# Filler products in gaps of TensorE, another order in the feed-forward slots, and a cast moved to GpSimd

## Chip, cores and metric

One core of a Trainium2 chip. The metric is the device time of one execution in microseconds, by the median of several executions. The profile comes from one further execution.

## The reference

The input is 32 images of 56 x 56 pixels with 24 channels, in float32. What is computed on it, one step after another:

- a Swin block: layer normalization, attention in shifted windows of 7 x 7 with 3 heads of 8, residual; then layer normalization, an MLP 24 to 96 to 24 with gelu, residual;
- a gated convolution block: `x + silu(conv3x3(h @ w_in) + conv_b)`, where `h` is the normalized input;
- twice (layers 0 and 1): `t + mixer(ln(t))`, where the mixer is a product 24 to 48 with batch norm and relu, an FFT over the 3136 tokens, a diagonal complex product with relu, the inverse FFT and a product 48 to 24; then `t + ffn(ln(t))`, where the ffn is 24 to 96 to 24 with relu on numbers rounded to an 8-bit float (5 exponent bits, 2 mantissa bits), accumulated to a 16-bit one:

```python
h = jax.nn.relu(_qlinear(x, W1, b1))
y = _qlinear(h, W2, b2)
```

## The kernel before

The 32 images are eight "quads" of 4 images; the 4 images of a quad lie side by side on the 128 partitions (32 each, 24 of them channels), the tokens in the free dimension. The loop over the quads is written out for each engine (`for q in range(nq)`), and the order in every engine's queue is written by hand; engines meet through semaphores that count up. A quad goes through window attention, MLP, convolution, and for each of two layers `mixer` and `ffn`.

Almost every matmul is recorded at one line, L1124 (`mm`), so its groups are told apart by tiles. `blocks` makes a product with a block-diagonal matrix as two products of 64 x 64. A float32 product shows as two records, so that `x4` is one call of `blocks` or two filler products. The eight PSUM banks are `ps[:, 0..7]`.

**Layer normalization** is a pipeline over four engines: TensorE subtracts the mean with a matrix (`center`), ScalarE squares (L695, for pairs L693), TensorE sums the squares (`variance`), ScalarE takes logarithm (L707, for pairs L705) and exponential with -0.5 (L712), VectorE multiplies (L932, for pairs L940, `normed`). TensorE's waits for these are the gaps that the change is about.

**Fillers.** `keep_busy(bank, n)` issues n full products of 128 x 128 by 128 x 448 into a bank that nobody reads. Before, it is called in four places: once in `mixer` ahead of the wait for the last normalized tile, with 2 products in each layer, once in `ffn` before the first up product (2), and for each late slot of layer 0 (1).

**The head of window attention.** TensorE waits for the first windows' scores' inputs: keys masked by head on VectorE (L982). Later each row of windows needs the row maxima: turned by TensorE, copied by ScalarE (L763), and written by 4 DMAs of the SP queue (L510).

**MLP.** For each of 8 rows of windows, two up products (96 rows out), gelu on ScalarE (L778), a down product. The last row's normalization is made at `i == 1`, between the first row's up products and the others.

**Convolution.** Normalization over four pairs, 2 x 9 taps of 16 products in two groups of rows, silu as exponential, logarithm and exponential on ScalarE (L793, L799, L803), `move` that turns the images back, residual on VectorE, then the centering of the mixer's normalization, pair by pair (`center_mix`), and their variances.

**Feed-forward slots.** `ffn` runs in 10 slots for 7 tiles of 448 tokens. In slot s TensorE issues, in this order: the mixer's last product for tile s (bank 7, `ps<-area_hz,mix`; VectorE adds it to `xs`, L1073), the variance for tile s-1, the variance of a second normalization that runs along (in layer 0 that of the next mixer, three tiles behind, in layer 1 that of the next quad's windows, one behind), the down product for tile s-2 (waits for `f_hid` and for VectorE's add), the up products for tile s-1 (three, wait for `normed`), the centering for tile s, and the centering of the second normalization. ScalarE copies the three up products to float16 (L841), the down product too (L833); VectorE adds bias and rectifies (L1097), casts all three parts, 1344 elements a partition, to the 8-bit float (L1103, `f_hid`), adds the down bias (L1086) and the residual (L1090). `r16` has one buffer: the next tile's rectification waits for `f_hid`; `hq8` has two.

**GpSimd** zeroes areas and the convolution's border, copies the pixels from window order to image order during the MLP (L632), and in quad 0 makes the tables of the transform (L593, L597), which it stores by DMA. SP loads them back (L500). Its queue per quad: border, eight copies, `input_pads` twice, `zero_ring` when the layer 1 inverse stage begins, `ones_in_ring`, `zero_key_pads` at the end.

Of the kernel before, what the change touches and what calls it, by code (L numbers as in the profile page):

```python
# [85 lines left out]
def LN_FFN(l):  # L86
    return 4 + 2 * l
# [177 lines left out]
def build_kernel(nc, x, keep, raw, g2, g4, out, nq=NQ):  # L265
    ctx = ExitStack()
    with ctx:
# [271 lines left out]
        def _(gp):  # L539
# [68 lines left out]

            for q in range(nq):
# [29 lines left out]
                input_pads()  # L639
                gp.wait_ge(filled, q * FILLS + step_of(1, ST_I2))  # L640
# [4 lines left out]
                gp.wait_ge(ring_ready, 2 * q + 3)  # L645
                gp.wait_ge(filled, q * FILLS + FILLS)
# [215 lines left out]
        def _(ve):  # L862
# [202 lines left out]
            def ffn(q, l):  # L1065
                o = l * (HC + 1)
                for s in range(FFN_SLOTS):
# [23 lines left out]
                    if 0 <= s - 1 < NT:  # L1091
                        b, k = (s - 1) % 2, l * NT + s - 1
                        for m in range(HC):
                            ve.wait_ge(f_half, (q * 2 * NT + k) * HC + m + 1)
                            if m == 0 and k >= 1:
                                ve.wait_ge(f_hid, q * 2 * NT + k)
                            ve.tensor_scalar(r16[:, m, :], a16[:, b, m, :], fb[:, o + m:o + m + 1],  # L1097
                                             0.0, ALU.add, ALU.max).then_inc(f_relu, 1)
                        ve.wait_ge(f_relu, (q * 2 * NT + k + 1) * HC)
                        if k >= 2:  # L1100
                            ve.wait_ge(f_down, q * 2 * NT + k - 1)
                        ve.sem_inc(passed_ve, 1)
                        ve.tensor_copy(hq8[:, b, :, :], r16, saturate=False).then_inc(f_hid, 1)  # L1103
# [18 lines left out]
        def _(pe):  # L1122
# [67 lines left out]
            def window_attention(q):  # L1190
# [8 lines left out]

                pe.wait_ge(normed, q * LN_N + NW)  # L1200
# [101 lines left out]
            def mlp(q):  # L1302
                pe.wait_ge(w2_loaded, 16 * HC)
                for i in range(NW + 1):
                    if i < NW:
                        row = MLP_ORDER[i]
                        if i == 1:
                            pe.wait_ge(attended, q * NW + NW)
                            center(q, LN_WIN2, NW - 1, xw)
                            variance(q, LN_WIN2, NW - 1)  # L1310
                        pe.wait_ge(normed, ln_count(q, LN_AT[LN_WIN2, row]))
# [21 lines left out]
            def conv(q):  # L1333
# [59 lines left out]
                center_conv(3)  # L1393
                pe.wait_ge(border, q + 1)
# [18 lines left out]
                center_mix(0)  # L1413
                center_mix(1)
# [8 lines left out]
            def mixer(q, l):  # L1423
# [18 lines left out]
                keep_busy(5 if l else 1, 2)  # L1442
# [85 lines left out]
            def ffn(q, l):  # L1528
                for s in range(FFN_SLOTS):
                    if s < NT:  # L1530
# [15 lines left out]
                    if 0 <= s - 1 < NT:  # L1546
                        variance(q, LN_FFN(l), s - 1)
# [222 lines left out]
```

## Time and profile before

| what | value |
|---|---|
| time, median of 3 runs | 3570.37 us (3561.97 to 3577.15) |
| profiled execution, its time | 3580.5 us |
| its span | 3578.7 us |
| TensorE (PE) busy | 3075.6 us, 86% |
| VectorE (DVE) busy | 1806.6 us, 50% |
| ScalarE (ACT) busy | 1622.2 us, 45% |
| GpSimd (POOL) busy | 215.0 us, 6% |
| granted TensorE clock, mean | 0.962 of full speed |

The profile is one execution. Rows of stretches give the stretch, its length, each engine's busy time with its number of instructions, the mean granted clock (PEclk) as a share of 2.4 GHz, the share of the DMA engines and GB/s. A timeline gives start, length, engine, line, operation, out<-in, the number of merged instructions and, in brackets, the idle time before and what ended it. PE is TensorE. Quads begin their attention at 47, 511, 948, 1385, 1826, 2262, 2697 and 3136 us.

### The profile page before, as it was taken

The page shows a single profiled execution, that of the slowest core. Times are in us where ns is not written, and L with a number is a line of the kernel's source. Part 1 is how long each engine was busy: PE and PEld are TensorE (multiplying, and loading weights), DVE is VectorE, ACT ScalarE, POOL GpSimd, SP SyncE. Part 2 cuts the span into 40 slices and gives each one's busy share as a digit, 9 for nine tenths or more (in the row PEclk, how much of TensorE's full clock was granted, in tenths as well). Part 3 has the DMA queues.
Part 4 walks back from the last instruction along what each step waited for, and adds up shares of the span by engine and source line. Part 5 has one row for each costly group of instructions (what it writes and reads, how often), then busy time and mean ns, then how long its engine had stood idle before and what let it go on. Part 6 is the DMA issues. An engine that isn't in the chain of part 4 may idle for free.

```text
span 3578.7 us, 110016 instructions
## 1 busy us (share of the span) xinstructions
PE 3075.6 (86%) x48976; PEld 1956.8 (55%) x48976; DVE 1806.6 (50%) x2852; ACT 1622.2 (45%) x2883; POOL 215.0 (6%) x462
## 2 busy tenths in 40 slices
PE   6968889788898888988989889888889888888888
PEld 3536646467354574554745647547465464554744
DVE  5524555355643546445464445634556355553555
ACT  2542354533555425544355443453544535435344
POOL 4510000000000000000000000000000000000000
PEclk8989999999999999999999999999999999999999
DMA  2321000110001100110001100011000110001100
GB/s 78 66 49 49 2 15 4 49 31 2 16 19 40 25 2 16 32 41 10 2 16 32 49 2 2 17 50 31 2 2 17 50 31 1 5 14 32 31 1 15
DMA packets 31251, 84.81 MB, mean 24 GB/s; under 512 B 24818, under 2 KB 25954, under 8 KB 26930
## 3 DMA queue, kind: packets, MB, share of 16 engines
q1 hardware_dynamic: 29506, 72.56, 8.5%
q8 instruction: 395, 6.47, 0.8%
q0 software_dynamic: 1280, 5.21, 0.5%
q14 instruction: 70, 0.57, 0.1%
HBM read 61.70 MB, written 14.84 MB: 21 GB/s over the span
## 4 chain that ended last, share of the span: by engine, by line
PE 72%; ACT 11%; DVE 6%; issue 5%; SPq 4%; DMA 3%; ACTq 0%; DVEq 0%
PE ps L1124 72%; ACT rs L712 3%; ACT lv L707 3%; SPq L495 2%; DMA area_ty<-area_hz 2%; SPq L510 1%; DVE area_ty L932 1%; DMA area_hz<-f_all 1%; DVE xs L1090 1%; ACT area_ty L793 1%; ACT area_ty L799 1%; ACT sq L693 1%; DVE area_ty L1086 1%; DVE area_ty L1062 0%; ACT lv L705 0%
## 5 line engine op out<-in xcount | busy, mean ns | idle before, releaser
L1124 PE MATMUL ps<-area_hz 32*64 32x147 f32 (+2 forms) x7180 | 365.2, 290 | 92.0 <-DVE area_hz L982 31.8
L1124 PE MATMUL ps<-area_ty,area_hz 113*64 113x49 f32 (+1 forms) x10240 | 393.8, 250 | 25.9 <-DMA area_ty<-area_hz 24.1
L1124 PEld LDWEIGHTS ps<-area_hz 32*64 32x64 f32 (+2 forms) x7180 | 293.2, 157 | 199.0 <-issue 175.5
L817 ACT ACTIVATE area_hz<-ps 121x384 f32<-121x384 f32 (+2 forms) x256 | 129.5, 519 | 590.6 <-PE ps L1124 590.6
L1124 PEld LDWEIGHTS ps<-area_ty,area_hz 113*64 113x64 f32 (+1 forms) x10240 | 332.4, 135 | 108.0 <-issue 107.4
L1124 PE MATMUL ps<-sq,keep_sb 64*64 64x392 f32 (+1 forms) x1728 | 328.5, 553 | 65.6 <-ACT sq L693 49.0
L932 DVE TENSOR_TENSOR area_ty<-ps,rs 128x392 f32<-128x392 f32 (+2 forms) x304 | 198.3, 653 | 327.0 <-ACT rs L712 326.9
L965 DVE TENSOR_REDUCE area_hz<-ps 113x12 f32<-113x588 f32 x256 | 196.7, 770 | 287.2 <-PE ps L1124 286.4
L1124 PE MATMUL ps<-area_ty,g_sb 56*112 56x192 f32 (+1 forms) x3712 | 311.5, 321 | 26.0 <-DVE area_ty L1062 19.7
L1124 PEld LDWEIGHTS ps<-area_ty,g_sb 56*112 56x112 f32 x3712 | 293.0, 173 | 44.7 <-issue 44.0
L1062 DVE COPY area_ty<-ps 120x896 f32<-120x896 f32 (+1 forms) x192 | 164.8, 858 | 255.8 <-PE ps L1124 255.8
L707 ACT ACTIVATE lv<-ps 128x448 f32<-128x448 f32 (+1 forms) x304 | 157.0, 517 | 275.4 <-PE ps L1124 275.4
L729 ACT ACTIVATE area_ty<-ps 113x588 f32<-113x588 f32 x256 | 168.8, 659 | 227.1 <-PE ps L1124 224.0
L817 ACT ACTIVATE area_ty<-ps 120x896 f32<-120x896 f32 (+1 forms) x192 | 140.2, 730 | 258.0 <-PE ps L1124 258.0
L1124 PE MATMUL ps<-xs,keep_sb 64*64 64x448 f32 (+1 forms) x1184 | 213.6, 538 | 47.1 <-DVE xs L1090 33.9
L1124 PEld LDWEIGHTS ps<-sq,keep_sb 64*64 64x64 f32 x1728 | 89.8, 138 | 288.4 <-ACT sq L695 122.4
L695 ACT ACTIVATE sq<-ps 128x448 f32<-128x448 f32 (+1 forms) x304 | 161.0, 529 | 177.0 <-PE ps L1124 172.2
L1124 PE MATMUL ps<-area_ty,ffn 128*128 128x448 fp8e5 x672 | 166.0, 355 | 86.2 <-DVE area_ty L932 81.9
L712 ACT ACTIVATE rs<-lv 128x448 f32<-128x448 f32 (+2 forms) x368 | 223.7, 608 | 32.7
L1124 PE MATMUL ps<-keep_sb,area_hz 112*58 112x56 f32 (+1 forms) x6144 | 196.2, 229 | 19.1 <-ACT area_hz L817 16.1
L1124 PEld LDWEIGHTS ps<-keep_sb,area_hz 112*58 112x58 f32 (+1 forms) x6144 | 193.6, 141 | 22.2 <-issue 22.1
L1124 PE MATMUL ps<-g_sb,area_ty 122*64 122x112 f32 (+1 forms) x3584 | 175.1, 259 | 12.5 <-issue 12.5
(123 smaller groups left out, 4078.9 us busy)
## 6 DMA issues: line engine op xcount, KB each, us to landing
area_hz<-f_all SPq DMA_DIRECT2D x16, 2541.0 KB
xw<-x_in SPq DMA_DIRECT2D x8, 1568.0 KB, 6.4
y_out<-xs SPq DMA_DIRECT2D x32, 252.0 KB
f_all<-piece POOLq DMA_DIRECT2D x16, 317.6 KB, 3.3
area_ty<-area_hz SPq DMA_DIRECT2D x256, 4.6 KB
area_hz<-raw_in SPq DMA_DIRECT2D x1, 2894.0 KB, 9.7
g_sb<-g_in SPq DMA_DIRECT2D x6, 355.2 KB
g_sb<-g_in SPq DMA_DIRECT2D x2, 710.5 KB
```

Source lines behind the costliest of these rows:

```text
L495: sp.dma_start(g4_sb[r + HALF * g:r + HALF * (g + 1), :, g, :], g4[r:r + HALF, :, :]).then_inc(tables_loaded, 16)
L510: sp.dma_start(qm[RW * j + 28:RW * j + 29, t % 3, :, :].rearrange("p w (h n) -> p (w h) n", n=L), mxt[NW * NH * g:NW * NH * g + NW * NH, t ...
L693: act.activation(halves(sq[:, k % 2, :]), pair_banks(i), ACT.Square).then_inc(squared, 1)
L695: act.activation(sq[:, k % 2, 0:w], ps[:, center_bank(k), 0:w], ACT.Square).then_inc(squared, 1)
L707: act.activation(lv[:, k % 2, 0:w], ps[:, variance_bank(k), 0:w], ACT.Ln).then_inc(logged, 1)
L712: act.activation(rs[:, k % 2, 0:w], lv[:, k % 2, 0:w], ACT.Exp, scale=-0.5).then_inc(root, 1)
L729: act.activation(pt[0:SIDE, n % 2, :, :], ps[0:SIDE, 2:4, 0:6 * L], ACT.Exp).then_inc(exped, 1)
L817: act.activation(dst, src, ACT.Relu if st in (ST_H, ST_F2) else ACT.Copy).then_inc(sc_kept, 1)
L932: ve.tensor_tensor(o, a, b, ALU.mult, **kw).then_inc(normed, 1)
L965: ve.tensor_reduce(mx[0:SIDE, u % 2, :].rearrange("p (g c r) -> p g c r", g=2, c=4)[:, :, k % 4], ps[0:SIDE, score_bank(k):score_bank(k) + ...
L1062: ins = ve.tensor_copy(dst, src)
L1124: return pe.matmul(o, a, b, start=start, stop=stop)
```

## The change

- `keep_busy` is called in five more places or with more products: 3 products at the head of window attention (quads 1 to 7), 1 and 2 in the MLP's step `i == 1`, 3 in the convolution after the last centering (behind a wait for the first pair's logarithm), 3 between the first two centerings of the mixer's normalization, and 4 for 2 in layer 0 of `mixer`. These are 14 products of a quad.
- In `ffn`, the variance for tile s-1 stands ahead of the mixer product for tile s.
- The cast of the rectified product moves from VectorE to GpSimd (`hidden_fp8`), with the same waits; layer 0's seven casts stand behind the second `input_pads`, layer 1's seven between the ring and the zeroing of the key columns.

```diff
--- before.py
+++ after.py
@@ -606,6 +606,16 @@
                 gp.memset(xhc[:, 0, HW + 1:64], 0.0)
                 gp.tensor_copy(xhc[:, 0, HW:HW + 1], spike[:, :]).then_inc(extra, 1)
 
+            def hidden_fp8(q, l):
+
+                for i in range(NT):
+                    k = l * NT + i
+                    gp.wait_ge(f_relu, (q * 2 * NT + k + 1) * HC)
+                    if k >= 2:
+                        gp.wait_ge(f_down, q * 2 * NT + k - 1)
+                    gp.sem_inc(passed_gp, 1)
+                    gp.tensor_copy(hq8[:, i % 2, :, :], r16, saturate=False).then_inc(f_hid, 1)
+
             for q in range(nq):
                 gp.wait_ge(attended, q * NW + NW)
                 gp.sem_inc(passed_gp, 1)
@@ -637,12 +647,14 @@
                 gp.wait_ge(filled, q * FILLS + step_of(0, ST_I1))
                 gp.sem_inc(passed_gp, 1)
                 input_pads()
+                hidden_fp8(q, 0)
                 gp.wait_ge(filled, q * FILLS + step_of(1, ST_I2))
                 gp.sem_inc(passed_gp, 1)
                 zero_ring()
                 gp.wait_ge(pads_ready, 3 + q + 1)
                 ones_in_ring()
                 gp.wait_ge(ring_ready, 2 * q + 3)
+                hidden_fp8(q, 1)
                 gp.wait_ge(filled, q * FILLS + FILLS)
                 gp.sem_inc(passed_gp, 1)
                 zero_key_pads()
@@ -1096,11 +1108,6 @@
                                 ve.wait_ge(f_hid, q * 2 * NT + k)
                             ve.tensor_scalar(r16[:, m, :], a16[:, b, m, :], fb[:, o + m:o + m + 1],
                                              0.0, ALU.add, ALU.max).then_inc(f_relu, 1)
-                        ve.wait_ge(f_relu, (q * 2 * NT + k + 1) * HC)
-                        if k >= 2:
-                            ve.wait_ge(f_down, q * 2 * NT + k - 1)
-                        ve.sem_inc(passed_ve, 1)
-                        ve.tensor_copy(hq8[:, b, :, :], r16, saturate=False).then_inc(f_hid, 1)
 
             for i in range(NW):
                 scale_windows(0, LN_FIRST, i)
@@ -1197,6 +1204,8 @@
                                  still[r, w, :], moving[r, w, :])
                     return ins
 
+                if q >= 1:
+                    keep_busy(2, 3)
                 pe.wait_ge(normed, q * LN_N + NW)
                 if q == 0:
                     pe.wait_ge(su_ve, N_SETUP_VE + 2)
@@ -1305,9 +1314,11 @@
                     if i < NW:
                         row = MLP_ORDER[i]
                         if i == 1:
+                            keep_busy(4, 1)
                             pe.wait_ge(attended, q * NW + NW)
                             center(q, LN_WIN2, NW - 1, xw)
                             variance(q, LN_WIN2, NW - 1)
+                            keep_busy(5, 2)
                         pe.wait_ge(normed, ln_count(q, LN_AT[LN_WIN2, row]))
                         for p in range(2):
                             u = 2 * i + p
@@ -1391,6 +1402,8 @@
                 variance_pair(LN_CONV, 1)
                 pe.wait_ge(mlp_added, q * NW + NW)
                 center_conv(3)
+                pe.wait_ge(logged, ln_count(q, LN_AT[LN_CONV, 0]))
+                keep_busy(0, 3)
                 pe.wait_ge(border, q + 1)
                 pe.wait_ge(normed, ln_count(q, LN_AT[LN_CONV, 1]))
                 tap(0, 0)
@@ -1411,6 +1424,7 @@
                     ins = tap(1, n)
                 ins.then_inc(conved, 1)
                 center_mix(0)
+                keep_busy(2, 3)
                 center_mix(1)
                 variance_pair(LN_MIX(0), 0)
                 move(1)
@@ -1439,7 +1453,7 @@
                 f3 = K("f3").rearrange("p (r n) -> p r n", r=2)
                 if l == 0:
                     pe.wait_ge(normed, ln_count(q, LN_AT[LN_MIX(0), 0]))
-                keep_busy(5 if l else 1, 2)
+                keep_busy(5 if l else 1, 2 if l else 4)
                 pe.wait_ge(normed, ln_count(q, LN_AT[LN_MIX(l), NT - 1 if l else NP - 1]))
                 pe.wait_ge(extra, q * 2 + l + 1)
                 for j in range(ST_STEPS[ST_H]):
@@ -1527,6 +1541,8 @@
 
             def ffn(q, l):
                 for s in range(FFN_SLOTS):
+                    if 0 <= s - 1 < NT:
+                        variance(q, LN_FFN(l), s - 1)
                     if s < NT:
 
                         if s >= 3:
@@ -1543,8 +1559,6 @@
                         pe.wait_ge(normed, ln_count(q, LN_AT[LN_WIN1, 0]))
                         pe.wait_ge(f_half, (q + 1) * 2 * NT * HC)
                         first_keys(q + 1)
-                    if 0 <= s - 1 < NT:
-                        variance(q, LN_FFN(l), s - 1)
                     if l == 0 and 0 <= s - 3 < NT:
                         variance(q, LN_MIX(1), s - 3)
                     if l == 1 and 0 <= s - 1 < NW:
```

## Rows read from the trace of the kernel before

**Rows 1.** Page, part 4; and the chain of waits, 196 to 290 us: start, us, what.

```profile
PE 72%; ACT 11%; DVE 6%; issue 5%; SPq 4%; DMA 3%; ACTq 0%; DVEq 0%
...
232.72 41.43 DMA area_hz<-f_all
```

**Rows 2.** Stretches of gelu, quads 1 and 7, and sum over quads 1 to 7.

```profile
633.56:651.78 18.22, 16.83 (x111) 3.83 (x108) 4.38 (x7) 12.15 (x16) 5.08 (x21) 0.72 0.42 92
...
3264.66:3280.04 15.38, 14.58 (x111) 3.78 (x108) 3.89 (x7) 12.15 (x16) 5.12 (x21) 0.89 0.51 109
sum 119.07, PE 110.41 PEld 27.51 DVE 29.80 ACT 85.45 POOL 35.72; mean PE 15.77 PEld 3.93 DVE 4.26 ACT 12.21 POOL 5.10
```

**Rows 3.** Stretches of the convolution, quad 7, and sum over quads 1 to 7.

```profile
3288.98:3308.85 19.87, 19.63 (x628) 11.08 (x631) 5.91 (x8) 8.24 (x10) 0.00 (x0) 1.00 0.02 4
sum 152.17, PE 145.45 PEld 80.60 DVE 41.39 ACT 57.70 POOL 0.00; mean PE 20.78 PEld 11.51 DVE 5.91 ACT 8.24 POOL 0.00
```

**Rows 4.** Stretches from the convolution to the mixer, sum over quads 1 to 7.

```profile
sum 132.79, PE 75.11 PEld 20.98 DVE 69.88 ACT 99.61 POOL 0.00; mean PE 10.73 PEld 3.00 DVE 9.98 ACT 14.23 POOL 0.00
```

**Rows 5.** Stretches of the mixer's first product, layer 0: quad 2, and sum.

```profile
1138.78:1148.93 10.15, 9.46 (x224) 9.29 (x225) 3.90 (x7) 3.43 (x7) 0.00 (x0) 1.00 0.02 4
...
sum 79.34, PE 74.46 PEld 73.34 DVE 27.32 ACT 24.02 POOL 0.00; mean PE 10.64 PEld 10.48 DVE 3.90 ACT 3.43 POOL 0.00
```

**Rows 6.** Stretch of window attention, quad 2.

```profile
947.95:1064.51 116.56, 110.40 (x2240) 73.81 (x2241) 63.93 (x85) 51.19 (x97) 0.00 (x0) 0.97 0.02 5
```

**Rows 7.** TensorE in order of time at the gaps: start, us, what [idle before].

```profile
1385.28 2.96 PE L1124 MATMUL ps<-area_hz 32*64 32x147 f32 x48 [3.53 <-DVE area_hz L982]
...
1503.19 0.88 PE L1124 MATMUL ps<-xw,keep_sb 64*64 64x392 f32 x4 [1.07 <-DVE area_ty L932]
...
1507.44 0.90 PE L1124 MATMUL ps<-area_ty,w 32*96 32x392 f32 x4 [1.91 <-DVE area_ty L932]
...
1533.84 0.97 PE L1124 MATMUL ps<-area_ty,wconv 32*32 32x392 f32 x16 [3.35 <-issue]
...
1563.04 1.22 PE L1124 MATMUL ps<-sq,keep_sb 64*64 64x392 f32 x8 [4.20 <-ACT sq L693]
...
1571.97 1.77 PE L1124 MATMUL ps<-keep_sb 128*128 128x448 f32 x4
1576.09 2.21 PE L1124 MATMUL ps<-mix,area_ty 64*64 64x96 f32 x36 [2.35 <-DVE area_ty L940]
```

**Rows 8.** Feed-forward slots: timelines of TensorE, ScalarE, VectorE, then the chain.

```profile
1354.61 0.96 PE L1124 MATMUL ps<-area_hz,mix 112*32 112x448 f32 x8
1355.50 1.63 PE L1124 MATMUL ps<-sq,keep_sb 64*64 64x448 f32 x8
...
1354.08 1.14 ACT L695 ACTIVATE sq<-ps 128x448 f32<-128x448 f32 x2
...
1355.67 0.68 DVE L1073 SCALAR_TENSOR_TENSOR xs<-ps,bn_bias,xs 128x448 f32<-128x448 f32 x1
...
1227.09 2.78 PE ps L1124 x16
...
1234.04 2.78 PE ps L1124 x16
...
1352.39 4.10 PE ps L1124 x23
...
1358.64 4.10 PE ps L1124 x23
```

**Rows 9.** Groups of GpSimd by shape: busy us, mean ns, idle before.

```profile
L593 POOL TENSOR_TENSOR piece<-terms,turns 121x672 f32<-121x672 f32 x32 | 45.9, 1455 | 49.0 <-DMA f_all<-piece 48.9
L597 POOL TENSOR_TENSOR piece<-piece 121x672 f32<-121x672 f32 x16 | 28.0, 1750 | 1.3
L632 POOL COPY xs<-xw 128x343 f32<-128x343 f32 x56 | 27.7, 495 | 123.7 <-issue 74.7 <-DVE xw L1022 49.0
L632 POOL COPY xs<-xw 128x28 f32<-128x28 f32 x56 | 11.6, 207 | 0.0
```

## Prediction

> **What bounds the kernel now.** I read the page first. The chain that ended last lies 72% on TensorE, with ScalarE and VectorE filling most of the rest: TensorE's stream, and the short waits inside it, set the time [rows 1]. That stream's speed depends on the granted clock, which is either 2.4 or 1.2 GHz. So the second view was stretches of one stage in quads 1 to 7, each with its mean granted clock as a share of 2.4 GHz. For a stretch of length T and mean clock c, the time at 1.2 GHz is 2(1-c)T. The gelu stretch of the MLP takes 18.22 us at 0.72 (10.2 us of it at 1.2 GHz) and 15.38 us at 0.89 (3.4 us) [rows 2]: 2.84 us for 6.8 us of low clock, or 0.42 us for each. The convolution takes 19.87 us with none [rows 3], and the first transform product of the mixer's layer 0 10.15 us with none [rows 5]. Third, TensorE's timeline, for what stands before such stretches: it idles 3.53 us before attention, 1.07 and 1.91 us in the MLP's head, 3.35 us before the taps, 4.20 us inside the second normalization and 2.35 us before the mixer [rows 7]. Fourth, one feed-forward slot. In layer 1 the mixer's last product (it fills bank 7) stands between the centerings and the variance at 1354.61, and the variance starts 0.89 us later at 1355.50, although the square it needs began at 1354.08 [rows 8].
>
> **Quad 0** gets nothing from the fillers: its mixer waits for the load of the table, 41 us that end at 274.15 [rows 1], so I count quads 1 to 7 for them and all eight for the slots.
>
> **Fillers, the cost.** One filler product is half of 1.77 us: two took that at 1571.97 [rows 7], so 0.88 us, 0.83 to the next start. Three before attention, 2.5 us, stand in 3.53 us of idleness that VectorE's masking ends; one (0.8) in 1.07, two (1.7) in 1.91; three (2.5) in 3.35, behind a wait for a logarithm that has ended when TensorE gets there; three (2.5) in 4.20; and two more (1.7) in 2.35 [rows 7]. All end before what ends the wait today, the closest with 0.2 us to spare. Cost: nothing. If a filler ran at 1.2 GHz it would take about 1.7 us instead of 0.8, and the three in the convolution would overrun by 1.7 us; fourteen in each of seven quads, all exposed, would be 7 x 14 x 0.83 = 81 us. I take 0 and keep a few us for the range.
>
> **Fillers, the gain,** if the clock stays at 2.4 GHz behind them. The full-clock length is subtracted from the sum over seven quads.
> - Gelu: 15.38 less 3.4 x 0.42 is 13.95; 119.07 - 7 x 13.95 = 21 us [rows 2]. ScalarE is busy 12.15 us of it, so a shorter floor than that isn't to be had.
> - Convolution: 152.17 - 7 x 19.87 = 13 us [rows 3]; 12 taken.
> - From there to the mixer: 132.79 us for seven, and 99.61 of it are ScalarE's [rows 4]. TensorE is not the bound, so I give half of the gelu rate, 0.2 us for each us, and 3.4 us of low clock a quad make 0.7 us: 4 us for seven, rounded down. Bounds 0 and 10.
> - First mixer product of layer 0: 79.34 - 7 x 10.15 = 8 us [rows 5].
> - Attention: one quad took 116.56 us at 0.97, 7.0 us of low clock, worth at most 2.9 us at the gelu rate [rows 6]. It has further waits, for the rows of maxima that come by DMA, that no filler is put into. I take 1 us a quad, 7 us; bounds 0 and 20.
> The sum is 52 us, with bounds 0 (no drop prevented) and 72. A change in the drops at other places, where the mixer's inverse stage starts, is not to be expected.
>
> **The slots.** Layer 1, one slot, with the order new. The square that begins at 1354.08 (two take 1.14 us) lets the variance start at 1354.71 instead of 1355.50. From the variance's start to the up products it is 3.14 us (1358.64 - 1355.50), which would give 1357.85. But the mixer product now follows the variance, 1355.51 to 1356.47, and VectorE adds it (0.68) until 1357.25, ahead of the normalization's scale in its order [rows 8]; that costs the scale 0.1, so 1357.94: 0.7 us less. Some is given back. The second variance is 0.9 us later against the first, so ScalarE reaches the second logarithm, the half-precision copies and the next square 0.23 us later, and the down product waits for the add. Followed round again the slot settles at 5.9 us instead of 6.25: four slots of 0.35, a first one of 0.6, a last one and the head that lose 0.3: **1.7 us a quad**. Layer 0: a slot is 6.95 us (1227.09 to 1234.04) and its loop goes through the second normalization: its variance now stands behind the mixer product, so its logarithm is 0.57 us later against the first variance, of the 0.89 us taken off: 0.32 gained, three times, 0.4 once before; the first, the last and the head lose 0.8 together, since there the square is not earlier or no mixer product was between: **0.5 us a quad**. Over eight quads 2.2 x 8 = 17 us. Bounds: 0 and 0.7 us for each of 96 slots, 67 us.
>
> **The cast.** It leaves VectorE, on whose queue nobody waits just behind it: in the new order the add that follows comes later still. Gain 0. On GpSimd the trace shows no cast. Its copies take 495 ns for 343 elements and 207 for 28: 0.91 ns an element and 0.18 us; 1344 elements would be 1.41 us. Its products of two tensors take 1455 and 1750 ns for 672: 2.9 and 3.5 us for 1344 [rows 9]. The bounds are a gain of 0 (a faster cast than 1.4 us has nobody waiting for it) and the cost at 3.5. I take 1.41, by the rows with one input and the same kind of operation. What waits for it is the down product of the next slot. In the layer 1 slot the rectifications end 2.6 us after the up products begin, the down product starts at 5.2: a cast of up to 2.1 us costs at most 5 us in all, at the tail; at 2.4 the slots still end 7 us under today's, at 2.9 they cost 30 us over today's, at 3.5 some 85 us. GpSimd's own queue: the zeroing of the key columns now stands behind the last cast, which ends 3 us before attention starts and takes 0.6; the zeroing of the ring (5.2 us) comes before the layer 1 slots. Both hidden.
> Weighed against a rule: the rows give GpSimd's copies 0.91 ns an element with one input [rows 9]. The Trainium skill, GPSIMD Engine Reference, section 3.1, gives 2.6 cycles an element at 1.2 GHz for elementwise work, which would be an estimated 2.9 us here; section 4.1 of the same page calls one-input work about line rate. By the first the slots would lose 30 us, by the second they gain 17; the first is rival 2.
> A second: in the rows the copies of GpSimd's setup vary, the in-place sum averages 1750 ns against 1455 for the product of the same size [rows 9], which a neighbour on VectorE may cause. The Trainium skill, SBUF - State Buffer, section Who interferes with whom, says that the two engines lock each other out of a shared port when VectorE reads two SBUF tensors. In my slot the cast (2.8 to 4.2 us after the up products) meets only VectorE's add from PSUM, so I charge nothing.
>
> **The sum.** 52 + 17 = 69 us off the profiled execution (3580.5 us, 3578.7 of them its span): 3511. The median of the runs, 3570.4, lies 10 us below that execution, so the forecast is 3502 us, 1.9% less.
>
> **Rivals.**
> 1. The fillers don't hold the clock, or it falls a few us later: only the slots' 17 us are left, 3553. For: the convolution's mean of 21.74 against 19.87 in quad 7 says that the same waits are not always followed by a drop, so more than their length counts [rows 3]. Against: what is left of each wait is 0.2 to 1.7 us. Chance 0.10.
> 2. The cast takes about 2.9 us, like the product of two tensors: the slots turn from -17 to +30, and the fillers' 52 stay: 3548. Chance 0.09.
> 3. Slower: the cast on the path of the next down product. From about 3.5 us (85 us on the slots, less 52) the kernel is slower, by 33 us: 3603; at 3.9 us it would be 3650. Place: TensorE waiting for GpSimd in front of each down product. For: the in-place sum's 2.6 ns an element would do it. Against: every one-input row. Chance 0.08.
> Forecast: 0.73.
>
> **The numbers.** A difference of 0.5% (18 us) is what a measurement of this kernel can tell from none. Faster by more: the forecast and most of rival 2, 0.73 + 0.09 = 0.82. Within: 0.10 (rival 1 lies on its edge). Slower: 0.08. The forecast's own range is 3478 (72 us from the fillers, 20 from the slots) to 3530; taken on to rivals 1 and 2 it is 3478 to 3554, which leaves rival 3 and the ends out.
>
> **What would show it.** Right: gelu stretches near 14 us with clock near 1.00, conv near 19.9, the mixer's first product at 10.15 in all quads, up products 5.9 us apart in layer 1 and 6.6 in layer 0, casts of 1.4 us on GpSimd, and no idle time on TensorE ended by GpSimd. Wrong: casts over 2.4 us; gaps after the fillers that end later than now; the clock still at 1.2 GHz in the gelu stretch.

## The result, and the profile after

The changed kernel takes 3513.0 us by the median of four runs, beside 3573.2 us for the kernel before (four runs as well, one more than the 3570.4 us of the forecast's table): a ratio of 0.984, with a 95% interval of 0.981 to 0.987. It is faster, by 1.6%; the forecast was 3502 us, 1.9% less, with a range of 3478 to 3554. The profiled execution's span fell from 3578.7 to 3515.2 us, 63.5 us.

First the page of the changed kernel, parts 1 and 4. `mm` is now line L1131.

```profile
PE 3115.1 (89%) x49194; PEld 1970.0 (56%) x49194; DVE 1704.2 (48%) x2740; ACT 1625.4 (46%) x2883; POOL 359.9 (10%) x574
...
PE 72%; ACT 12%; DVE 5%; issue 5%; SPq 4%; DMA 3%; ACTq 0%; DVEq 0%
```

The chain still lies 72% on TensorE, as in [rows 1]. TensorE is busy for 39.5 us more although the span is shorter. The 109 added filler products would be an estimated 90 us by 0.83 us each; the rest of its work takes some 50 us less, because less of it runs at 1.2 GHz. VectorE is busy for 102 us less and GpSimd for 145 us more, and VectorE's share of the chain went from 6 to 5%. The mean granted clock rose from 0.962 to 0.980.

Then the stages, as rows of stretches like those of [rows 2 to 6] (stretch, length, busy time and number of instructions of PE, PEld, DVE, ACT and POOL, granted clock, DMA share, GB/s). The gelu stretches of quads 1, 2 and 6, and the sum over quads 1 to 7:

```profile
631.08:646.45 15.37, 13.98 (x111) 3.64 (x108) 4.38 (x7) 12.14 (x16) 5.12 (x21) 0.89 0.50 109
1061.63:1075.44 13.81, 12.66 (x111) 3.82 (x108) 4.21 (x7) 12.14 (x16) 5.13 (x21) 1.00 0.56 121
...
2777.95:2794.61 16.66, 15.74 (x111) 4.11 (x108) 3.98 (x7) 12.14 (x16) 5.11 (x21) 0.80 0.47 100
...
sum 102.63, PE 94.35 PEld 26.33 DVE 29.56 ACT 84.99 POOL 35.81; mean PE 13.48 PEld 3.76 DVE 4.22 ACT 12.14 POOL 5.12
```

Four of seven quads run at 13.8 us and full clock. Quads 1, 4 and 6 still have 3.4, 3.4 and 6.8 us at 1.2 GHz (such a time is called a drop below). The convolution, quad 5 and the sum:

```profile
2368.38:2390.49 22.11, 20.73 (x628) 10.95 (x630) 5.91 (x8) 8.24 (x10) 0.00 (x0) 1.00 0.02 4
...
sum 143.71, PE 136.91 PEld 78.27 DVE 41.39 ACT 57.69 POOL 0.00; mean PE 19.56 PEld 11.18 DVE 5.91 ACT 8.24 POOL 0.00
```

The clock is 1.00 in all seven, yet quads 1, 3, 5 and 7 take 20.7 to 22.1 us, the others 19.8 or 19.9. From the convolution to the mixer, the sum; then the sum of the mixer's first product in layer 0:

```profile
sum 123.81, PE 94.21 PEld 30.65 DVE 70.04 ACT 99.63 POOL 0.00; mean PE 13.46 PEld 4.38 DVE 10.01 ACT 14.23 POOL 0.00
...
sum 71.06, PE 66.19 PEld 65.06 DVE 27.32 ACT 24.02 POOL 0.00; mean PE 9.46 PEld 9.29 DVE 3.90 ACT 3.43 POOL 0.00
```

Both stages are the same in every quad now (17.68 to 17.70, and 10.15 or 10.16). Attention, sum over quads 1 to 7, which was 819.45 us before (121.92 of them in quad 7, which takes 114.88 us now):

```profile
sum 812.00, PE 764.12 PEld 511.34 DVE 447.58 ACT 358.75 POOL 0.00; mean PE 109.16 PEld 73.05 DVE 63.94 ACT 51.25 POOL 0.00
```

TensorE in order of time, at the gaps of [rows 7] (what stands in brackets is the idle time that is left and what ended it):

```profile
1365.25 1.23 PE L1131 MATMUL ps<-area_hz 32*64 32x147 f32 x32 [1.27 <-DVE area_hz L994]
...
1084.38 0.95 PE L1131 MATMUL ps<-area_ty,wconv 32*32 32x392 f32 x32 [0.90 <-issue]
...
1109.92 0.89 PE L1131 MATMUL ps<-sq,keep_sb 64*64 64x392 f32 x8 [1.59 <-ACT sq L705]
...
1121.93 1.29 PE L1131 MATMUL ps<-mix,area_ty 64*64 64x96 f32 x26 [0.86 <-DVE area_ty L952]
```

Each of these gaps keeps idle time that the same instruction as before ends, and the MLP's head, from the end of attention to the gelu stretch, takes 6.80 us in both kernels: at full clock the fillers delay nothing. Last the slots. Stretches of layer 0's slots in quads 2 and 6, and one of layer 1's, of the kernel before (first fence) and of the changed one (second), each with the sum over eight quads:

```profile
1206.45:1264.47 58.02, 45.88 (x223) 12.67 (x223) 32.85 (x63) 34.53 (x70) 0.00 (x0) 1.00 0.00 1
...
sum 465.48, PE 370.46 PEld 102.11 DVE 262.84 ACT 276.54 POOL 0.00; mean PE 46.31 PEld 12.76 DVE 32.85 ACT 34.57 POOL 0.00
...
2209.26:2261.68 52.42, 42.73 (x230) 13.00 (x231) 32.18 (x65) 35.31 (x75) 0.60 (x1) 1.00 0.09 21
...
sum 423.25, PE 340.18 PEld 103.30 DVE 256.47 ACT 282.16 POOL 4.82; mean PE 42.52 PEld 12.91 DVE 32.06 ACT 35.27 POOL 0.60
```

```profile
1188.43:1245.57 57.14, 45.49 (x222) 12.56 (x222) 26.18 (x56) 34.88 (x70) 9.13 (x7) 1.00 0.00 1
...
2907.58:2966.12 58.54, 48.16 (x222) 13.12 (x223) 26.20 (x56) 34.99 (x70) 9.12 (x7) 0.94 0.00 1
sum 463.98, PE 376.52 PEld 103.10 DVE 209.61 ACT 279.57 POOL 72.99; mean PE 47.07 PEld 12.89 DVE 26.20 ACT 34.95 POOL 9.12
...
2173.17:2224.79 51.62, 45.72 (x237) 13.71 (x237) 25.95 (x58) 35.44 (x75) 9.69 (x8) 1.00 0.09 21
...
sum 415.57, PE 362.72 PEld 107.80 DVE 206.56 ACT 282.98 POOL 77.50; mean PE 45.34 PEld 13.48 DVE 25.82 ACT 35.37 POOL 9.69
```

At full clock layer 0 gains 0.9 us a quad and layer 1 0.8. But of layer 0's eight stretches five now have 3.4 or 6.8 us at 1.2 GHz; before, two had 3.4. GpSimd's casts, as the group of its line that answers to [rows 9]:

```profile
L617 POOL CAST area_ty<-area_ty 128x1344 fp8e5<-128x1344 f16 x112 | 146.1, 1305 | 870.2 <-DVE area_ty L1109 870.2
```

**Where the 63.5 us come from,** stage by stage: gelu 16.4, convolution 8.5, from there to the mixer 9.0, first product 8.3, attention 7.4, together 49.6; the slots 1.5 and 7.7 over eight quads; in quads 1 to 7 the rest of layer 0's mixer 4.1, where two fewer quads have a drop at the inverse stage (one for three), and layer 1's mixer -0.5 (five with a drop in both kernels). That is 62.4, and the rest is in quad 0.

### The profile page after: what moved, and what is told of

The parts are those of the page before. It is cut to its first block, busy times and chain, and to the rows that moved or that the text cites. A ratio compares the mean times of both kernels' runs of the same rounds, so it can differ in the third digit from the quotient of the medians.

```text
span 3515.2 us, 110460 instructions
## 1 busy us (share of the span) xinstructions
PE 3115.1 (89%) x49194; PEld 1970.0 (56%) x49194; DVE 1704.2 (48%) x2740; ACT 1625.4 (46%) x2883; POOL 359.9 (10%) x574
## 4 chain that ended last, share of the span: by engine, by line
PE 72%; ACT 12%; DVE 5%; issue 5%; SPq 4%; DMA 3%; ACTq 0%; DVEq 0%
PE ps L1131 72%; ACT lv L719 2%; SPq L495 2%; ACT rs L724 2%; ACT area_ty L853 2%; DMA area_ty<-area_hz 1%; ACT sq L707 1%; SPq L510 1%; DMA area_hz<-f_all 1%; DVE xs L1102 1%; ACT area_ty L845 1%; ACT sq L705 1%; DVE area_ty L1098 1%; ACT area_ty L805 1%; ACT area_ty L811 1%
## 5 line engine op out<-in xcount | busy, mean ns | idle before, releaser
L1131 PE MATMUL ps<-area_hz 32*64 32x147 f32 (+2 forms) x7180 | 357.7, 285 | 84.7 <-DMA area_hz<-f_all 28.8
L1131 PE MATMUL ps<-area_ty,area_hz 113*64 113x49 f32 (+1 forms) x10240 | 393.5, 250 | 22.1 <-DMA area_ty<-area_hz 20.1
L1131 PE MATMUL ps<-sq,keep_sb 64*64 64x392 f32 (+1 forms) x1728 | 335.1, 531 | 71.0 <-ACT sq L707 44.0
L1131 PEld LDWEIGHTS ps<-area_hz 32*64 32x64 f32 (+2 forms) x7180 | 287.8, 154 | 191.2 <-issue 168.7
L1131 PEld LDWEIGHTS ps<-area_ty,area_hz 113*64 113x64 f32 (+1 forms) x10240 | 332.0, 135 | 104.1 <-issue 103.5
L1131 PE MATMUL ps<-area_ty,g_sb 56*112 56x192 f32 (+1 forms) x3712 | 311.8, 321 | 26.0 <-DVE area_ty L1074 19.7
L1131 PEld LDWEIGHTS ps<-area_ty,g_sb 56*112 56x112 f32 x3712 | 293.3, 173 | 44.7 <-issue 44.0
L1131 PE MATMUL ps<-xs,keep_sb 64*64 64x448 f32 (+1 forms) x1184 | 219.8, 542 | 63.1 <-DVE xs L1102 48.0
L1131 PEld LDWEIGHTS ps<-sq,keep_sb 64*64 64x64 f32 x1728 | 84.1, 133 | 297.0 <-ACT sq L707 135.5
L617 POOL CAST area_ty<-area_ty 128x1344 fp8e5<-128x1344 f16 x112 | 146.1, 1305 | 870.2 <-DVE area_ty L1109 870.2
L1131 PE MATMUL ps<-keep_sb,area_hz 112*58 112x56 f32 (+1 forms) x6144 | 196.8, 229 | 17.7 <-ACT area_hz L829 16.0
L1131 PEld LDWEIGHTS ps<-keep_sb,area_hz 112*58 112x58 f32 (+1 forms) x6144 | 193.9, 141 | 21.1 <-issue 20.8
L1085 DVE SCALAR_TENSOR_TENSOR xs<-ps,bn_bias,xs 128x448 f32<-128x448 f32 x112 | 76.6, 684 | 233.7 <-PE ps L1131 233.7
```

What stands on the lines that cost most here:

```text
L617: gp.tensor_copy(hq8[:, i % 2, :, :], r16, saturate=False).then_inc(f_hid, 1)
L1085: ve.scalar_tensor_tensor(xs[:, sl], ps[:, 7, 0:TT], bn_bias[:, l:l + 1], xs[:, sl], ALU.add, ALU.add).then_inc(ve_kept, 1)
L1131: return pe.matmul(o, a, b, start=start, stop=stop)
```

## Experiments

**The theory** is the prediction's: the fillers hold the clock, the order in the slots gives a little, the cast gives nothing. **Rivals:** the order or the cast brings more than that; or drops are not prevented but only moved.

### The three parts, each alone or taken back

`e1_order` is the kernel before with only the variance put first:

```diff
                 for s in range(FFN_SLOTS):
+                    if 0 <= s - 1 < NT:
+                        variance(q, LN_FFN(l), s - 1)
...
-                    if 0 <= s - 1 < NT:
-                        variance(q, LN_FFN(l), s - 1)
```

> The kernel before with the variance ahead of the mixer product alone. My theory, corrected by the trace of after: the feed-forward stages of layer 0 shorten from 58.0 to about 57.2 us and those of layer 1 from 52.4 to about 51.7, 1.5 us a quad, 12 us in all (ratio 0.9967), and the granted clock stays where it was (0.96). Rival, that the order gives nothing by itself and the fillers made the whole gain: ratio 1.000. Rival, that the slots pay the whole 0.7 us they save at first order: 96 x 0.7 = 67 us, ratio 0.981.

Measured: 0.998 (0.997 to 0.999), 3563.5 us beside 3570.9. Two of its layer 0 slot stretches, quads 6 and 7, and the sum over eight:

```profile
2946.38:3005.09 58.71, 48.32 (x222) 13.13 (x223) 32.20 (x63) 35.03 (x70) 0.00 (x0) 0.94 0.00 1
3381.95:3439.10 57.15, 45.49 (x223) 12.59 (x223) 32.21 (x63) 34.91 (x70) 0.00 (x0) 1.00 0.00 1
sum 467.87, PE 382.37 PEld 104.57 DVE 257.76 ACT 280.00 POOL 0.00; mean PE 47.80 PEld 13.07 DVE 32.22 ACT 35.00 POOL 0.00
```

In quad 7, at full clock, the order takes 58.02 to 57.15, as in the changed kernel; layer 1 is 51.63 in six quads. So the order alone is worth 0.87 + 0.79 = 1.7 us a quad, 13 us. But seven of eight layer 0 stretches now have low clock in their last slots, and their sum is higher than before (467.87 us for 465.48). By the slots of this execution 4.9 us are left of the 13; by the medians the order is worth 7.3 us. So about half of its gain goes through the clock. That step was missing from the prediction.

`e2_cast` is the kernel before with only the cast moved (`hidden_fp8` on GpSimd, the five lines out of VectorE's):

> The kernel before with the cast on GpSimd alone. Theory: the cast was waited for by nobody and still is not, 0 us (ratio 1.000), casts of 1.3 us, feed-forward stages of 58.0 and 52.4 us unchanged except for up to 0.3 us at the tail of layer 1. Rival, that the move helps by freeing VectorE (98 us less busy): ratio below 0.998. Rival, that the later cast delays the down products: ratio above 1.002.

Measured: 1.000 (0.999 to 1.001). The slot stretches at full clock stay at 58.01 and 52.43 us. VectorE had nobody waiting behind the cast. `e4_cast_back` takes the cast back from the changed kernel:

> The kernel after with the cast back on VectorE. Theory: within 5 us of after (ratio to before about 0.984), since in the new order the add of the mixer product comes long after the cast in either place; if anything the tails are 0.1 us shorter. Rival, that the cast on VectorE holds up the add or the scale in the shorter slots: feed-forward stages longer by 0.3 us or more a slot-loop, ratio 0.99 or more.

Measured: 0.986 (0.984 to 0.988), 3517.8 us; its slots take 57.18 and 51.61 us at full clock, within 0.04 us of the changed kernel's. The cast's place is worth nothing in either kernel.

`e3_fill` is the kernel before with all fillers and nothing else:

```diff
+                if q >= 1:
+                    keep_busy(2, 3)
...
+                            keep_busy(4, 1)
...
+                            keep_busy(5, 2)
...
+                pe.wait_ge(logged, ln_count(q, LN_AT[LN_CONV, 0]))
+                keep_busy(0, 3)
...
+                keep_busy(2, 3)
...
-                keep_busy(5 if l else 1, 2)
+                keep_busy(5 if l else 1, 2 if l else 4)
```

> The kernel before with the five filler places alone. Theory: they carry some 45 us of the 60 (ratio about 0.987), the time at 1.2 GHz in gelu, convolution and up to the mixer's first product falls to some 10 us or less over the quads 1 to 7, and no gap ends later than before. Rival, that the fillers only pay with the shorter slots, or that the order pays most: ratio 0.995 or more.

Measured: 0.988 (0.986 to 0.990), 3524.3 us, 47 us less, with a clock of 0.983. Its sums: gelu 101.4, convolution 142.7, to the mixer 123.8, first product 71.1, attention 809.4, none above the changed kernel's by more than 0.1. This part carries four fifths of the change. The drops themselves can be counted: in each of the three traces without the new fillers (the kernel before, `e1_order`, `e2_cast`) all seven quads have one at the gelu stretch, and there are 15 to 17 from there to the end of the mixer's first product. With the fillers the gelu stretch has 3 (this run and the changed kernel), 0 (`e4_cast_back`) and 1 (`e5_cast_twice`, at its end), and from there on there are 0 or 1.

### How much filler it takes

`e11_one` is the changed kernel with one product in each place instead of three, two, three and three, and three instead of four in the mixer.

> The kernel after with 1 product instead of 3, 2, 3 and 3 in its filler places and 1 more instead of 2 in the mixer (the first MLP filler stays). Theory: what the clock answers to is how much of a wait is left idle, so with 2.5 us and more left in the waits before attention, in the convolution and in the second normalization the drops come back there, in about half of the quads, and the ratio to before lies between after's 0.984 and the order's 0.998, near 0.990. Rival, that any product in the gap is enough: 0.984.

Measured: 0.990 (0.988 to 0.992), clock 0.973. Its sums of gelu, of the convolution and from there to the mixer:

```profile
sum 108.60, PE 99.61 PEld 26.08 DVE 30.11 ACT 85.00 POOL 35.76; mean PE 14.23 PEld 3.73 DVE 4.30 ACT 12.14 POOL 5.11
...
sum 146.94, PE 140.01 PEld 80.39 DVE 41.37 ACT 57.71 POOL 0.00; mean PE 20.00 PEld 11.48 DVE 5.91 ACT 8.24 POOL 0.00
...
sum 131.95, PE 87.42 PEld 24.95 DVE 69.86 ACT 99.62 POOL 0.00; mean PE 12.49 PEld 3.56 DVE 9.98 ACT 14.23 POOL 0.00
```

From the convolution to the mixer nearly the whole gain is gone (131.9 against 123.8, and 132.8 in [rows 4]); gelu keeps 10 of 16 us, the convolution 5 of 8. So one product is not enough in any of the three, but how much it brings differs: much in gelu, where it takes the place of two, nearly nothing ahead of the mixer, where it takes the place of three.

### The cast doubled

`e5_cast_twice` is the changed kernel with one more copy of 1344 elements on GpSimd (121 partitions, into `twin`, a part of a tile that nobody needs then) ahead of each cast:

```diff
+                    gp.wait_ge(f_hid, max(1, q * 2 * NT + k)) if q or k else None
...
+                    gp.tensor_copy(twin, r16[0:121].rearrange("p m n -> p (m n)"))
                     gp.tensor_copy(hq8[:, i % 2, :, :], r16, saturate=False).then_inc(f_hid, 1)
```

> The kernel after with a copy of the same 1344 elements on GpSimd ahead of each cast (into an area nobody reads), so that the cast is ready 1.3 us later. Theory of rivals 2 and 3 of the prediction: the down product waits from about 2.1 us on; at 2.65 us the slots lose about 3 us a quad against after, 25 us in all (ratio to before about 0.991), and TensorE's idle time shows GpSimd as releaser. Rival, that there is more slack than I worked out: within 5 us of after (0.984). Rival, that every slot pays the copy in full: 96 x 1.3 = 125 us, ratio 1.02.

Measured: 0.984 (0.982 to 0.986), the changed kernel's own ratio. By the total the copies would cost nothing. The groups of GpSimd and one layer 1 slot stretch say otherwise:

```profile
L621 POOL CAST area_ty<-area_ty 128x1344 fp8e5<-128x1344 f16 x112 | 146.4, 1307 | 0.0
L620 POOL COPY piece<-area_ty 121x1344 f16<-121x1344 f16 x112 | 146.3, 1307 | 751.8 <-DVE area_ty L1113 751.8
```

```profile
2174.07:2226.87 52.80, 45.55 (x236) 13.74 (x237) 26.13 (x58) 35.68 (x75) 18.46 (x15) 1.00 0.09 22
```

Layer 1's slots take 52.80 against 51.62 us, alike in quads 1 to 6; layer 0's 57.44 against 57.14 in the one quad at full clock. That is 1.5 us a quad, some 12 us. The 12 us came back elsewhere: attention 807.6 (812.0), gelu 99.1 (102.6), layer 1's mixer, all quads, 537.1 (541.8), where two inverse stages have a drop and not six. Whether the copy has a part in that, or only chance, no run shows. An edit of 10 us can't be priced by the total while drops are about; stretches at full clock can. The prediction's curve gave 25 us for a cast of 2.6 us: too steep.

### The drops that are left

Two more edits go after them. `e6_tail` puts more fillers in the last slots of layer 0, and takes bank 0 for them instead of 4:

```diff
-                    if l == 0 and s > NT:
-                        keep_busy(4, 1)
+                    if l == 0 and s >= NT:
+                        keep_busy(0, 2 if s == NT + 1 else 1)
```

> The kernel after with filler products in the last slots of layer 0: 1 where there was none (slot 7) and 2 for 1 (slot 8). In after the clock falls there in 5 of 8 quads. Theory: those drops go, the layer 0 stage is 57.15 us in all quads instead of 58.0 on average, 5 to 8 us less than after (ratio to before about 0.982). Rival, that the fillers delay the centerings behind them: layer 0 stages above 57.2 at full clock.

`e7_more` adds to it one filler in the wait for the MLP's first gelu and one in two rows of attention:

```diff
+                            if u == 3:
+                                keep_busy(6, 1)
...
+                        if q >= 1 and n in (0, 4):
+                            keep_busy(5, 1)
```

> e6 and two more places: one filler between the two up products of the MLP's second row (a wait of 0.63 us for gelu, so it overruns by 0.2) and one ahead of the first two waits for rows of maxima in window attention. Theory: gelu stretches 14.0 us in all quads (three of after's were 15.4 to 16.7), attention 114 to 115 us instead of 116 on average: 10 to 15 us less than e6 (ratio to before about 0.978). Rival, that what makes the clock fall in gelu are the narrow products and not the waits: the drops stay, ratio as e6.

Measured: `e6_tail` 0.980 (0.979 to 0.982), `e7_more` 0.979 (0.977 to 0.981), clock 0.988. The layer 0 slots of `e6_tail`, sum over eight quads, then the gelu stretch of `e7_more`, quad 6 and sum:

```profile
sum 457.33, PE 375.95 PEld 106.59 DVE 209.56 ACT 279.03 POOL 73.00; mean PE 46.99 PEld 13.32 DVE 26.20 ACT 34.88 POOL 9.12
```

```profile
2760.22:2774.28 14.06, 13.54 (x113) 3.97 (x110) 4.21 (x7) 12.16 (x16) 5.12 (x21) 1.00 0.54 116
...
sum 98.46, PE 94.80 PEld 27.80 DVE 29.47 ACT 85.16 POOL 35.74; mean PE 13.54 PEld 3.97 DVE 4.21 ACT 12.16 POOL 5.11
```

All eight slot stretches are at 57.2 and full clock: fillers hold it there as well, and 6.7 us come back (463.98 to 457.33). More came than was looked for: layer 1's mixer, the next stage, takes 532.4 us for 541.8, since none of its eight inverse stages has a drop in this execution, where six had. `e7_more` has the same fillers there and two drops, so this second part isn't sure. In the gelu stretch the filler costs 0.25 us at full clock (14.06 for 13.81) and takes away what was left, 102.6 to 98.5. The two in attention did little: 806.8 us beside 808.3 in `e6_tail`, 115.3 a quad, where 114 to 115 were expected, and the intervals of the two versions overlap.

`e8_inverse` goes on from `e7_more`, with a filler ahead of the inverse stage:

```diff
+                pe.wait_ge(ve_kept, q * VE_FILLS + vector_fills(step_of(l, ST_F2, FOLDS)))
+                keep_busy(0, 1)
```

> e7 and one filler product between the last forward and the first inverse transform product of each mixer, in a wait of about 1 us that VectorE and ScalarE end. In after the clock falls there in 9 of 16 mixers, 1.55 us each. Theory: it falls no more, the stretches from the first transform product to the feed-forward slots take 56.35 us in both layers instead of 57.3 on average in e7, 10 us less in all (ratio to before about 0.976). Rival, that the narrow products of the inverse stage and not the wait bring the clock down there: unchanged, or slower by 16 x 0.1 us.

Measured: 0.981 (0.979 to 0.983), no better. TensorE in order of time at that place, first in `e7_more`, then in `e8_inverse`:

```profile
1156.07 1.03 PE L1131 MATMUL ps<-area_ty,g_sb 56*112 56x96 f32 x16 [0.39 <-issue]
1158.10 4.12 PE L1131 MATMUL ps<-keep_sb,area_hz 112*64 112x56 f32 x83 [1.01 <-ACT area_hz L829]
```

```profile
1157.36 1.03 PE L1131 MATMUL ps<-area_ty,g_sb 56*112 56x96 f32 x16 [0.39 <-issue]
1159.27 1.02 PE L1131 MATMUL ps<-keep_sb 128*128 128x448 f32 x2 [0.88 <-DVE area_hz L1067]
1160.22 2.99 PE L1131 MATMUL ps<-keep_sb,area_hz 112*64 112x56 f32 x96
```

The drop is gone: from quad 0's second mixer on no inverse stage has low clock. But VectorE's folds, which the filler waits for, end almost when the wait itself does: the filler starts 1.91 us after the last product's start, the inverse stage of `e7_more` 2.03. Behind the filler it is 2.86. The stretch from layer 0's first product to its slots takes 57.2 us in each quad, instead of 56.3 without a drop or 57.9 with one. In `e7_more` six of fifteen mixers (quad 0's first left out) had a drop: 6 x 1.55 = 9 us to gain, and 15 x 0.86 = 13 us to pay.

### The order on ScalarE

In layer 1's slots TensorE waits for the square, which ScalarE takes up behind four copies. `e9_scalar_order` is `e7_more` with ScalarE's copy of the down product put behind the square, and VectorE's rectification ahead of the down bias, in layer 1:

```diff
-                    if 0 <= s - 2 < NT:
+                    if l == 0 and 0 <= s - 2 < NT:
...
+                    if l == 1 and 0 <= s - 2 < NT:
+                        k = l * NT + s - 2
+                        act.wait_ge(f_down, q * 2 * NT + k + 1)
```

> e7 with another order in the layer 1 slots: ScalarE squares the centered tile before it copies the down product, and VectorE rectifies before it adds the down product. In after TensorE waits 0.44 us a slot for that square. Theory (what the slot of layer 1 lacks is ScalarE's turn and not TensorE's time): slots of 5.6 to 5.7 us instead of 6.05, stage of layer 1 at 49.8 instead of 51.6, 12 to 14 us less than e7 (ratio to before about 0.975). Rival, that TensorE's own products and VectorE's add in front of the down product already bind: within 3 us of e7.

`e10_both` is this together with `e8_inverse`:

> e8 and e9 together. If both theories hold, 22 us less than e7, ratio to before about 0.972; if the clock at the inverse stage stays, as e9.

Measured: 0.977 (0.975 to 0.979) and 0.977 (0.975 to 0.979), 3488.0 and 3486.5 us. Layer 1's slots of `e9_scalar_order`, quads 6 and 7:

```profile
3006.06:3056.12 50.06, 45.76 (x237) 13.62 (x237) 32.50 (x58) 36.06 (x75) 9.79 (x8) 1.00 0.06 11
3430.06:3485.07 55.01, 42.23 (x222) 11.76 (x222) 31.15 (x57) 35.31 (x73) 9.79 (x8) 0.95 0.10 23
```

51.6 becomes 50.05 us in quads 1 to 6, and over eight quads it is 405.7 us for 415.5, 9.8 us less where 12 to 14 were expected; in the last quad 53.9 becomes 55.0, where no next quad's work runs along and the end comes behind the last down product's copy; that this copy is the cause is argued only. Both are the fastest versions here, and beat the changed kernel; their intervals overlap with that of `e7_more`. `e10_both` has no drop at the inverse stages either and still adds nothing to `e9_scalar_order`: its forecast of 0.972 failed at the filler that starts too late, as in `e8_inverse`.

## Why the prediction held, and where it missed

**The direction and the mechanism** held: `e3_fill` alone gives 47 of the some 58 us, by the clock. The sum was 69 us off a profiled execution, and 63.5 were measured. That it is so near is in part luck: gelu, convolution and slots together bring 15.9 us less than their terms, the way to the mixer, first product and attention 5.7 more, and 4.7 come from stages that had no term. Rival 1 (the fillers don't hold the clock) falls with `e3_fill`. Rivals 2 and 3 (a cast of 2.9 or 3.5 us) fall with 1.305 us, and no idle time of TensorE is ended by the cast.

**Fillers, the cost:** taken as nothing, and in every gap looked at above it is; the convolution is the one place where that is open.

**Gelu:** 21 us predicted, 16.4 measured. The floor was right (13.81; 13.95 was worked out), but I took the drop as gone in all quads and three still have it, a number that varies between executions (none in `e4_cast_back`). With one more product none of the seven quads has it, in the traces of `e7_more`, `e8_inverse` and `e9_scalar_order` alike.

**Convolution:** 12 predicted, 8.5 measured, though no drop is left. What failed is that 19.87 us was taken as its length at full clock; here every second quad has 20.7 or more, 4.8 us in all above 19.85, in part with short waits between the taps. One of the four such waits in quad 5 of the changed kernel, in TensorE's order of time:

```profile
2377.39 3.65 PE L1131 MATMUL ps<-area_ty,wconv 32*32 32x392 f32 x126 [0.37 <-issue]
```

"issue" names no releaser, and no run is aimed at it: its cause is open. It goes with the fillers: in all four traces with just those of the change (changed kernel, `e3_fill`, `e4_cast_back`, `e5_cast_twice`) quads 1, 3, 5 and 7 take 20.4 to 22.1 us and the others 19.8 or 19.9, all at full clock; in the three without them the seven stretches that have no drop, quads 1, 3 and 7 among them, take 19.8 to 20.3. So a cost of the fillers of 3 to 5 us in all, which the prediction didn't have, isn't excluded.

**From the convolution to the mixer:** 4 predicted with a bound of 10, and 9.0 measured. Half of the gelu rate was too low. ScalarE's busy time is the same (99.63 us for 99.61) and the stretch is 1.3 us shorter, so TensorE's speed was on the path although ScalarE is the busiest. The chain of waits shows where: between two of ScalarE's squares stood 5.6 us of TensorE's work, most of them at 1.2 GHz in this quad; now it is two pieces of TensorE's work with VectorE's addition between them, 3.7 us together. Quad 4, before and after:

```profile
2002.28 5.56 PE ps L1124 x56
```

```profile
1967.86 1.73 PE ps L1131 x35
...
1969.61 1.05 DVE xs L1050 x2
...
1970.70 0.93 PE ps L1131 x8
```

**First product:** 8 and 8.3.

**Attention:** 7 and 7.4, but as 1 us a quad it didn't come: 7.0 of the 7.4 us are quad 7's, and single quads still vary from 114.0 to 119.0. That the three products at the head bring something shows over the traces: 815.6 to 819.5 us in the three without them, 807.6 to 812.2 in the five that have them and no others in attention.

**"A change in the drops at other places, where the mixer's inverse stage starts, is not to be expected"** is the sentence that was wrong. In layer 0's last slots quads with a drop went from two to five, and to seven with the order alone. At the inverse stages themselves it is about the same number (eight before, seven after), at other quads. One trace a kernel would be little for that, but they agree: with the old order two, two and three quads have such a drop (before, `e2_cast`, `e3_fill`), with the new one seven, five, five and seven (`e1_order`, changed kernel, `e4_cast_back`, `e5_cast_twice`). So the order brings them, and `e6_tail` shows that fillers in the last slots remove every one. Why the order brings them is open: TensorE's busy share of the stretch is no lower than before (45.49 of 57.14 us against 45.88 of 58.02).

**The slots:** 17 us predicted, 9.2 measured, 13.4 at full clock (eight times 0.86 and 0.81). Layer 0 was 0.9 instead of 0.5 a quad, layer 1 0.8 instead of 1.7. Layer 0's slots are 6.6 us as forecast, so it is the 0.8 us taken off for its first slot, its last and the head that were too much. In layer 1 the slots settle at 6.05 us where I had 5.9, because TensorE waits 0.44 us for ScalarE's square; and I missed, at the head, that the two old filler products and the second variance come before the first up products: TensorE itself delays these, which start 7.57 us after the stretch does, 7.36 before. TensorE in order of time, first slots of quad 2 in layer 1:

```profile
1318.80 0.88 PE L1131 MATMUL ps<-sq,keep_sb 64*64 64x392 f32 x4
1319.60 1.77 PE L1131 MATMUL ps<-keep_sb 128*128 128x448 f32 x4
1321.21 0.73 PE L1131 MATMUL ps<-area_ty,ffn 128*128 128x448 fp8e5 x3
...
1329.55 0.97 PE L1131 MATMUL ps<-sq,keep_sb 64*64 64x448 f32 x4 [0.44 <-ACT sq L707]
```

**The cast:** 1.41 us by the rows of GpSimd's copies, 1.305 measured, 0.97 ns an element. The copies were the right neighbour to take, and the product of two tensors the wrong one. The Trainium skill, GPSIMD Engine Reference, section 3.1, has 2.6 cycles an element, by which it would have been an estimated 2.9 us; but the same section gives that figure as the floor of work with two inputs, so the prediction read it too widely. Section 4.1 of the same page has one-input work at about line rate, and the measurement agrees with it. Of a shared port the runs can say little. In the changed kernel none of the 112 casts overlaps an instruction of VectorE. In `e2_cast` 80 run beside the addition from PSUM, and in `e5_cast_twice` 97 beside that or the normalization's scale; all of them still take 1.30 or 1.31 us. In none of the three kernels does a cast meet VectorE's residual addition, the one with both inputs in SBUF.

## What to carry to other kernels

Where a float32 kernel's stages take two lengths with two granted clocks, the waits ahead of them are worth filling with products into an unread bank, as long as they end before what ends the wait; fill most of the gap, since one product where two or three fit gave from nearly nothing to two thirds of the gain, and put none where it can only start when the wait is nearly over. Look afterwards for stages where drops have appeared: another order can lose through the clock what it gained. Price edits of ten microseconds by stretches at full clock, and not by the total.

## What was not expected of the hardware

The clock can fall where hardly anything is idle. TensorE in quad 1 of the changed kernel, in order of time, and then the stretches around the fall:

```profile
627.73 0.88 PE L1131 MATMUL ps<-sq,keep_sb 64*64 64x392 f32 x4 [0.59 <-ACT sq L707]
628.53 1.77 PE L1131 MATMUL ps<-keep_sb 128*128 128x448 f32 x4
630.51 0.90 PE L1131 MATMUL ps<-area_ty,w 32*96 32x392 f32 x4 [0.21 <-DVE area_ty L944]
632.04 2.81 PE L1131 MATMUL ps<-area_ty,w 32*96 32x392 f32 x16 [0.63 <-ACT area_ty L790]
```

```profile
624.00:633.40 9.40, 7.85 (x42) 2.36 (x38) 1.50 (x3) 6.15 (x10) 0.45 (x4) 1.00 0.66 144
633.40:636.80 3.40, 3.40 (x23) 0.61 (x16) 0.63 (x1) 1.90 (x3) 0.78 (x3) 0.50 0.69 152
```

No wait there is longer than 0.63 us and the engine is busy for 7.85 of 9.40 us, yet the clock is at 1.2 GHz from 633.4 on for 3.4 us. In quad 2 the waits ahead are the same 0.21 and 0.63 us and nothing falls. What decides between the two was not found; with one more product in the 0.63 us wait (`e7_more`) no quad has the fall in its gelu stretch.
